# Source and key lists kept in SBUF, and a ScalarE copy in place of each group's index DMA

## The chip, the cores and the metric

The kernel runs on one core of a Trainium2 chip. The metric is the device time of one execution in microseconds (us), and less is better. Engines are called as in the profile: PE (TensorE matmul, with its weight loads as PEld), DVE (VectorE), ACT (ScalarE), POOL (GpSimd) and SP (SyncE, which here only issues DMAs). A "q" behind a name is that engine's sequencer: waits, register work, DMA issues.

## The reference

Four graph layers over 12,500 nodes with 64 features and 200,000 edges (`src`, `dst`), each followed by a residual sum and a layer norm. The edges are sorted by `dst`.

```python
# layer 0: weighted mean of neighbours
msg = x[src] * edge_weight[:, None];            agg = segment_sum(msg, dst)
# layer 1: messages with edge features
msg = relu(x[src] + edge_attr);                 agg = segment_sum(msg, dst)
# layer 2: x_i and x_j - x_i through one linear map, batch norm, leaky relu
msg = concat([x[dst], x[src] - x[dst]]) @ W.T + b;   h = segment_sum(msg, dst)
# layer 3: graph attention, 8 relations
h = x @ W[r]; s = h @ a_src; d = h @ a_dst
e = leaky_relu(s[src] + d[dst]); alpha = segment_softmax(e, dst)
out += segment_sum(alpha[:, None] * h[src], dst) + bias[r]
```

## The kernel before

The edges are cut into G = 196 groups of 1,024 (128 partitions by S = 8). Each layer begins with a pass over all groups that gathers the rows of the source nodes and sums them by destination. These are passes 0, 1, 2 and 3; a later pass reads back what pass 3 kept, and dense stages stand between the passes. Every pass is a loop of IT = 49 turns with Q = 4 groups in a turn, and group g uses slot q = g mod 4 of `gat` (gathered rows) and `idx` (eight int32 row numbers on each partition).

A gather pass works like this:

- **POOL** (`gather_pass`) waits until the slot's row numbers are there (`s_idx[q]`) and the slot is free (`s_free[q]`), and issues eight indirect DMAs (line 486), one for each of the eight columns. Each of them fetches 128 rows.
- **SP** (`refill`, line 286) waits for `s_free[q]` and then loads the next row numbers of that slot, a DMA of 4 KB from `src_p`, or from `key_d` in pass 3. `first_indices` (line 292) does so for the first four groups of passes 1 to 3.
- **DVE and PE** consume a group. In passes 0 to 2 DVE multiplies or adds (L1005, L1058), makes a one-hot matrix of the destinations in two halves (L931), PE multiplies it with the messages (L679, 8 matmuls), and DVE adds the result to `sum_t` (L937). One `p_sum` bank and one `oh` buffer are used, so that these steps follow each other. The slot is freed by DVE after L1005 (pass 0), by ACT after its Relu (L563, pass 1) or by DVE after the sum (pass 2).
- **Pass 3** has two chains that share no data. ACT waits for a group's gathers, stores the slot to `he_d` (L623), copies one column into `trip` (L625) and then frees the slot of the group before (`free_slot`). DVE and PE meanwhile work from the destination row `drow`: a one-hot by nodes (L1193), 8 matmuls (L793), a selection (L1196, L1200) and a sum (L1202), for each "window" of 128 nodes that the group touches, 293 windows in all. SP feeds both chains in a fixed order: for each group it waits for `s_drused` (DVE has finished a group), issues `dst_row` (L396), then waits for `s_free[q]` and issues the index DMA.

The code that sets this order on SP in pass 3:

```python
def pass3(it, final):
    for q in range(Q):
        if not (final and q >= Q - 2):
            wait_reg(sp, s_drused, it * Q + (q + 1))
            dst_row(q % 2, it * Q + (q + 2))
        if not final:
            refill(3, q, it, key_d)
```

The kernel's functions that the diff touches:

Of the kernel before, what the change touches and what calls it, by code (L numbers as in the profile page):

```python
# [5 lines left out]
P, S = 128, 8  # L6
# [3 lines left out]
Q = 4  # L10
# [26 lines left out]
def program(nc, x, src_p, dst_p, type_p, weight_p, dst_f, type_f, edge_attr, weights, out):  # L37
# [5 lines left out]
    he_d = dram("he_d", (G, P, S * HROW))  # L43
    key_d = dram("key_d", (P, G, S), i32)
    dst16_d = dram("dst16_d", (EP,), i16)
# [4 lines left out]
    with ExitStack() as ctx:  # L50
# [49 lines left out]
        src_i, type_i, dst_i = [trip_flat.bitcast(i32)[:, k * T:(k + 1) * T] for k in range(3)]  # L100
        dstn_i = scan_flat.bitcast(i32)[:, 0:T]
        dst16 = scan_flat[:, 2 * T:2 * T + T // 2].bitcast(i16)
        stat_i = oh[0:SG, :, :, :].rearrange("p a s w -> p (a s w)")[:, 0:2 * GE].bitcast(i32)
# [158 lines left out]
        def _(sp):  # L262
            flat = "p g s -> p (g s)"
            sp.dma_start(stat_i, dst_f.rearrange("(a g e) -> g a e", a=2, g=SG)).then_inc(s_load[0], 16)
            sp.dma_start(dst_i, dst_p.rearrange(flat)).then_inc(s_load[1], 16)
# [23 lines left out]
            def first_indices(n, source):  # L289
                for q in range(Q):  # L290
                    sp.wait_ge(s_free[q], IT * n + 1)
                    sp.dma_start(idx[:, q, :], source[:, q, :]).then_inc(s_idx[q], 16)

# [72 lines left out]

            with sp.Fori(0, IT - 1) as it:
                for q in range(Q):
                    refill(0, q, it, src_p)
            sp.wait_ge(s_keyst, 32)  # L370
            dense_io(0)

            first_indices(1, src_p)
            ea_d = edge_attr.rearrange("(g p s) d -> g p (s d)", p=P, s=S)
# [3 lines left out]
            with sp.Fori(0, IT - 1) as it:  # L378
                for q in range(Q):
                    refill(1, q, it, src_p)  # L380
# [4 lines left out]
            first_indices(2, src_p)  # L385
            with sp.Fori(0, IT - 1) as it:
                for q in range(Q):
                    refill(2, q, it, src_p)
            dense_io(2)
            dense_io(3)  # L390
            dense_io(4)

            first_indices(3, key_d)

# [72 lines left out]
        def _(pool):  # L467
# [27 lines left out]
            pool.wait_ge(s_table, 4)  # L495
            pool.wait_ge(s_keyst, 32)
            gather_pass(3, rel_d, HROW)
# [29 lines left out]
        def _(act):  # L527
            def square_root(n, b, k, per):
# [5 lines left out]
                else:  # L534
                    nc.scalar.activation(r1[:, :], r1[:, :], ACT.Sqrt).then_inc(s_sqrt[n], 1)

            act.wait_ge(s_vconst, 2)
            act.wait_ge(s_sum[0], 1)
# [20 lines left out]

            with act.Fori(0, IT) as it:  # L560
                for q in range(Q):
                    wait_reg(act, s_pre, it * Q + (q + 1))
                    nc.scalar.activation(msg[:, q % 2, :, 0:D], ea[:, q, :, :], ACT.Relu).then_inc(s_msg, 1)  # L563
                    wait_reg(act, s_msg, it * Q + (G + q + 1))
                    act.sem_inc(s_free[q], 1)

            def hidden(it, u, b):
# [51 lines left out]

            with act.Fori(0, IT) as it:  # L620
                for q in range(Q):
# [5 lines left out]
                    if q:  # L627
                        free_slot(q - 1, it)
                free_slot(Q - 1, it)
            act.wait_ge(s_scan_copy, G)  # L630
            act.sem_inc(s_trip, 1)
# [212 lines left out]
        def _(dve):  # L844
# [21 lines left out]
            ch.start()  # L866
            dve.wait_ge(s_load[0], 16)
            ch.add(vec.tensor_reduce(out=ends_g[:, 0, :], in_=stat_i, op=ALU.min, axis=AX.X))
# [10 lines left out]
            dve.sem_inc(s_cols, 1)  # L879
            dve.wait_ge(s_load[1], 16)  # L880
            vec.memset(dstf[:, G, :], 0.0)
# [34 lines left out]

            dve.wait_ge(s_load[3], 48)
# [565 lines left out]
```

## Time and profile before

| | us |
|---|---|
| median of 3 runs (12548.62 to 12606.76) | 12603.83 |
| the profiled execution, by the same clock | 12571.97 |
| its span | 12570.2 |
| busy in it: POOL / PE / DVE / ACT | 6491.1 / 3621.9 / 3237.4 / 329.6 |

The span is 1.8 us shorter than the execution's own time. POOL's busy time counts an indirect DMA as busy for as long as POOL makes its descriptors. No engine is busy for more than 52% of the span. So the page's first part does not say what limits the kernel, and the four gather passes have to be read one by one.

### The profile page before, as it was taken

The numbers are of one execution on the slowest core, as the hardware profiler recorded it, in microseconds if no ns is written. First come the engines' busy times: TensorE is split into PE (matmuls) and PEld (weight loads), VectorE is DVE, ScalarE is ACT, GpSimd is POOL, SyncE is SP. The second block draws the span as 40 slices with busy tenths as digits, with TensorE's granted clock in tenths as the row PEclk, the third lists the DMA queues.
The fourth block names the chain that finished last, engine by engine and source line by source line (L and its number), as shares of the span: only waits on it lengthen the run. The fifth ranks groups of instructions, "written<-read, shape, count | busy, mean of one in ns | idle before, by whom it ended". The sixth has DMA issues, their size and how long they took to land.

```text
span 12570.2 us, 99249 instructions
## 1 busy us (share of the span) xinstructions
PE 3621.9 (29%) x17244; PEld 2968.1 (24%) x17245; DVE 3237.4 (26%) x5805; ACT 329.6 (3%) x648; POOL 6491.1 (52%) x6716
## 2 busy tenths in 40 slices
PE   2222222242222222432232223640000000003558
PEld 2222222242222222322222222220000000002555
DVE  2111211141111111221111111322222222286554
ACT  0000000010000000000000000100000000000000
POOL 6666666525556566346666665035555555402443
PEclk6555555555555555555555555555555555556885
DMA  1111111111111111111111111232222222302220
GB/s 41 21 21 21 20 21 21 20 37 40 40 41 41 41 42 41 37 27 22 22 22 22 22 22 23 65 100 64 64 65 65 64 66 66 64 0 48 72 71 19
DMA packets 620736, 509.88 MB, mean 41 GB/s; under 512 B 405721, under 2 KB 405721, under 8 KB 620574
## 3 DMA queue, kind: packets, MB, share of 16 engines
q0 software_dynamic: 200704, 212.34, 9.2%
q1 hardware_dynamic: 391778, 239.40, 7.5%
q10 hardware_dynamic: 28224, 57.82, 1.2%
q8 instruction: 9, 0.15, 0.0%
q14 instruction: 21, 0.17, 0.0%
HBM read 405.06 MB, written 103.99 MB: 40 GB/s over the span
## 4 chain that ended last, share of the span: by engine, by line
another core or an unknown queue 32%; issue 21%; DVE 16%; DVEq 15%; PE 14%; ACT 1%; DMA 1%; POOL 0%; ACTq 0%; POOLq 0%; SPq 0%; PEldq 0%
PE p_sum L679 6%; DVEq L213 5%; DVE oh L931 3%; DVEq L931 2%; DVE oh L945 2%; DVEq L926 1%; DVEq L209 1%; PE p_a L777 1%; DVEq L1193 1%; DVEq L1189 1%; DVE sel L1196 1%; DVE sel L1200 1%; DVE msg L1005 1%; PE p_sum L834 1%
## 5 line engine op out<-in xcount | busy, mean ns | idle before, releaser
L486 POOL DMA_INDIRECT gat<-x_d,idx x3136 | 3034.9, 968 | 2241.3 <-DMA idx<-in_src_p 1272.4
L679 PE MATMUL p_sum<-oh,msg 128*66 128x128 f32 (+1 forms) x6272 | 1410.8, 418 | 3681.1 <-DVE oh L931 1676.8
L486 POOL DMA_INDIRECT gat<-rel_d,idx x1568 | 1492.0, 952 | 1612.6 <-DMA idx<-key_d 1079.3
L679 PEld LDWEIGHTS p_sum<-oh,msg 128*66 128x66 f32 (+1 forms) x6272 | 1269.7, 227 | 3821.7 <-DVE oh L931 2910.5
L486 POOL DMA_INDIRECT gat<-in_x,idx x1568 | 1532.4, 977 | 1001.8 <-DMA idx<-in_src_p 526.5
L937 DVE TENSOR_TENSOR sum_t<-sum_t,p_sum 64x128 f32 (+1 forms) x588 | 165.0, 281 | 5204.9 <-remote 4100.1
L679 PE MATMUL p_sum<-oh,gat 128*64 128x128 f32 x3136 | 687.5, 410 | 1723.1 <-DVE oh L931 1184.6
L679 PEld LDWEIGHTS p_sum<-oh,gat 128*64 128x64 f32 x3136 | 616.6, 219 | 1793.8 <-DVE oh L931 1219.6
L931 DVE SCALAR_TENSOR_TENSOR oh<-dstf,fine_col,iota 128x512 f32<-128x512 f32 x1176 | 835.0, 748 | 510.2 <-issue 406.1
L793 PE MATMUL p_sum<-trip_s,oht 128*128 x2344 | 202.0, 237 | 2410.9 <-DVE oht L1193 1255.6
L793 PEld LDWEIGHTS p_sum<-trip_s,oht 128*128 128x128 bf16 x2344 | 168.8, 166 | 2445.6 <-issue 2445.6
L811 PE MATMUL p_sum<-oh,msg 128*72 128x128 f32 x3136 | 460.2, 310 | 866.3 <-POOL msg L508 862.2
L811 PEld LDWEIGHTS p_sum<-oh,msg 128*72 128x72 f32 x3136 | 412.6, 166 | 913.8 <-issue 913.8
L506 POOL TENSOR_TENSOR msg<-gat,edge_w 128x512 f32<-128x512 f32 x196 | 205.0, 1046 | 771.0 <-DMA gat<-he_d 527.7
L1196 DVE TENSOR_TENSOR sel<-p_sum,toh 128x384 f32<-128x384 f32 x293 | 163.4, 558 | 877.7 <-remote 451.8
L1193 DVE TENSOR_SCALAR oht<-drow,node_col 128x1024 bf16<-128x1024 int16 x293 | 148.6, 507 | 624.1 <-issue 456.9
L945 DVE SCALAR_TENSOR_TENSOR oh<-dstf,fine_col,iota 128x512 f32<-128x512 f32 x394 | 277.6, 744 | 4.9
L508 POOL TENSOR_TENSOR msg<-toh,edge_w 128x64 f32<-128x64 f32 x196 | 124.9, 637 | 239.3 <-DVE oh L945 239.3
L1058 DVE TENSOR_TENSOR ea<-ea,gat 128x512 f32<-128x512 f32 x196 | 136.4, 696 | 231.2 <-issue 228.1
L563 ACT ACTIVATE msg<-ea 128x512 f32<-128x512 f32 x196 | 123.4, 630 | 2421.3 <-DVE ea L1058 2150.5
L834 PE MATMUL p_sum<-w_wcat,xt 64*128 64x512 f32 x196 | 172.4, 1069 | 0.0
L777 PE MATMUL p_a<-w_wcat,xt 64*128 64x512 f32 x196 | 172.1, 1067 | 0.0
(240 smaller groups left out, 3061.1 us busy)
## 6 DMA issues: line engine op xcount, KB each, us to landing
he_d<-gat ACTq DMA_DIRECT2D x196, 288.0 KB
gat<-he_d SPq DMA_DIRECT2D x196, 288.0 KB, 2.8
ea<-in_edge_attr SPq DMA_DIRECT2D x196, 256.0 KB
gat<-x_d,idx POOLq DMA_INDIRECT x3136
drow<-dst_d SPq DMA_DIRECT2D x196, 256.0 KB
rel_d<-sum_t SPq DMA_DIRECT2D x14, 2016.0 KB, 6.4
gat<-in_x,idx POOLq DMA_INDIRECT x1568
gat<-rel_d,idx POOLq DMA_INDIRECT x1568
```

The source lines that it names most:

```text
L213: v = eng.value_load(win[0:1, table, bass.ds(g, 1)], min_val=0, max_val=(NW * G << 16) - 1)
L486: nc.gpsimd.indirect_dma_start(out=gat[:, q, s, 0:width], out_offset=None, in_=table, in_offset=bass.IndirectOffsetOnAxis(ap=idx[:, q, s:s ...
L506: nc.gpsimd.tensor_tensor(msg[:, q % 2, :, 0:D], gat[:, q, :, 0:D], by_tile(alpha, D), ALU.mult)
L679: ins = nc.tensor.matmul(p_sum[0:width, 0, 0:W], lhs(q, s), oh[:, 0, s, :], start=(s == 0), stop=(s == S - 1))
L777: ins = nc.tensor.matmul(p_a[:, k, :], tile(xt, u, t, D), wt["wcat"][:, :], start=True, stop=True)
L793: ins = nc.tensor.matmul(p_sum[:, 0, s * 6 * R:(s + 1) * 6 * R], oht_tile[:, :, s], table, start=True, stop=True)
L811: ins = nc.tensor.matmul(p_sum[0:HROW, u, 0:W], msg[:, u, s, :], oh[:, u, s, :], start=(s == 0), stop=(s == S - 1))
L834: ins = nc.tensor.matmul(p_sum[:, k, :], tile(xt, u, t, D), wt["wcat"][:, :], start=True, stop=True)
L931: vec.scalar_tensor_tensor(out=oh[:, 0, h * half:(h + 1) * half, :], in0=bc(dst.unsqueeze(2), P, half, W), scalar=fine_col[0:P, bass.ds(at ...
L945: ins = vec.scalar_tensor_tensor(out=oh[:, u, h * half:(h + 1) * half, :], in0=bc(dst.unsqueeze(2), P, half, W), scalar=fine_col[0:P, bass ...
L1193: vec.tensor_scalar(oht[:, :], drow[:, q % 2, :], node_col[:, bass.ds(w, 1)], None, ALU.is_equal).then_inc(s_oh[3][0], 1)
L1196: ch2(vec.tensor_tensor(sel[:, :, :, :].rearrange("p s c (k r) -> p s (c k) r", k=3), p_sum[0:P, 0, 0:S * 6 * R].rearrange("p (s c r) -> p ...
```

## The change

The lists of all source rows (`src_i`) and of all keys (source times 8 plus type, now `key_i`, which has a place of its own in `trip_s`) stay in SBUF. They have 1,568 int32 on each partition. The 784 index DMAs of SP are gone, and so is the round trip of the keys through `key_d`. ACT now waits for `s_free[q]` and copies the group's eight columns into `idx[:, q, :]`; the copy counts `s_idx[q]` up by 1. POOL waits for `s_idx[q]` alone. In passes 0 and 2 ACT does nothing else (`all_indices`); in pass 1 the copy stands behind the Relu of the same slot, in pass 3 behind `free_slot`. On SP the waits for `s_free` remain in pass 1 only, ahead of the load of `edge_attr`. The source list is the first DMA of the program.

```diff
+            sp.dma_start(src_i, src_p.rearrange(flat)).then_inc(s_load[1], 16)
...
-            for q in range(Q):
-                sp.dma_start(idx[:, q, :], src_p[:, q, :]).then_inc(s_idx[q], 16)
-            sp.dma_start(src_i, src_p.rearrange(flat)).then_inc(s_load[3], 16)
...
-            sp.dma_start(key_d.rearrange(flat), src_i).then_inc(s_keyst, 16)
...
-            def refill(n, q, it, source):
-
-                wait_reg(sp, s_free[q], it + (2 + IT * n))
-                sp.dma_start(idx[:, q, :], source[:, bass.ds(it * Q + (Q + q), 1), :]
-                             .rearrange("p a s -> p (a s)")).then_inc(s_idx[q], 16)
...
                     if not (final and q >= Q - 2):
                         wait_reg(sp, s_drused, it * Q + (q + 1))
                         dst_row(q % 2, it * Q + (q + 2))
-                    if not final:
-                        refill(3, q, it, key_d)
...
-                        wait_reg(pool, s_idx[q], it * 16 + 16 * (1 + IT * n))
-                        wait_reg(pool, s_free[q], it + (1 + IT * n))
+                        wait_reg(pool, s_idx[q], it + (1 + IT * n))
...
+            def give_indices(n, q, it, rows_of):
+
+                wait_reg(act, s_free[q], it + (1 + IT * n))
+                nc.scalar.activation(idx[:, q, :], rows_of[:, bass.ds(it * (Q * S) + q * S, S)], ACT.Copy)\
+                    .then_inc(s_idx[q], 1)
...
+            act.wait_ge(s_load[1], 16)
+            all_indices(0)
...
                     nc.scalar.activation(msg[:, q % 2, :, 0:D], ea[:, q, :, :], ACT.Relu).then_inc(s_msg, 1)
                     wait_reg(act, s_msg, it * Q + (G + q + 1))
                     act.sem_inc(s_free[q], 1)
+                    if not final:
+                        give_indices(1, q, act.snap(it + 1), src_i)
...
+            all_indices(2)
...
                     if q:
                         free_slot(q - 1, it)
+                        if not final:
+                            give_indices(3, q - 1, act.snap(it + 1), key_i)
                 free_slot(Q - 1, it)
+                if not final:
+                    give_indices(3, Q - 1, act.snap(it + 1), key_i)
...
-            ch.add(vec.scalar_tensor_tensor(out=src_i, in0=src_i, scalar=float(R), in1=type_i, op0=ALU.mult, op1=ALU.add))
+            ch.add(vec.scalar_tensor_tensor(out=key_i, in0=src_i, scalar=float(R), in1=type_i, op0=ALU.mult, op1=ALU.add))
```

Two places show how the queues change. The first is SP in the loop of pass 3. Before the change, half a turn of it reads (L396 is `dst_row`, L286 the index DMA; an ISA or REGISTER_ALU row is register work, with the wait that stands on it):

```order
L396 ISA [waits s_drused]
L396 DMA drow<-dst_d 128x1024
L209 REGISTER_ALU
L286 ISA [waits s_free0]
L286 DMA idx<-key_d 128x8
L396 ISA [waits s_drused]
L396 DMA drow<-dst_d 128x1024
L286 ISA [waits s_free1]
L286 DMA idx<-key_d 128x8
```

After it the same stretch reads (`dst_row` is line 371 there):

```order
L385 ISA
L371 ISA [waits s_drused]
L371 DMA drow<-dst_d 128x1024
L371 ISA [waits s_drused]
L371 DMA drow<-dst_d 128x1024
```

The index load has left the queue in which it stood behind the wait for DVE, and `dst_row` no longer stands behind the wait for a free slot.

The second place is ACT in the same loop. Before the change (L623 is the store, L625 the copy into `trip`):

```order
L623 ISA [waits s_gat1]
L623 DMA he_d<-gat 128x576
L625 ISA
L625 ACTIVATE trip<-gat 128x8
L209 ISA [waits s_scan_copy]
L623 ISA [waits s_hest0,s_gat2]
L623 DMA he_d<-gat 128x576
```

After it (the store is line 621, the copy into `trip` 623, the index copy 511):

```order
L621 ISA [waits s_gat1]
L621 DMA he_d<-gat 128x576
L623 ISA
L623 ACTIVATE trip<-gat 128x8
L208 ISA [waits s_scan_copy]
L208 REGISTER_ALU [waits s_hest0]
L511 ISA [waits s_free0]
L511 ACTIVATE idx<-trip_s 128x8
L621 ISA [waits s_gat2]
L621 DMA he_d<-gat 128x576
```

The index copy of slot 0 for the next turn stands right behind the freeing of slot 0 and ahead of the wait for the gathers of slot 2. No instruction of DVE or PE is waited for between them.

## Rows read from the trace of the kernel before

**Rows 1.** Stretches of the four gather passes: length, busy us (count), PEclk, DMA share, GB/s

```profile
11.00:2537.00 2526.00, 705.92 (x3126) 634.12 (x3127) 507.65 (x1018) 0.00 (x0) 1532.43 (x1568) 0.57 0.12 22
2718.00:5228.00 2510.00, 685.01 (x3072) 617.47 (x3072) 453.45 (x768) 120.88 (x192) 1520.15 (x1568) 0.57 0.18 41
5423.00:7813.00 2390.00, 681.09 (x3104) 610.95 (x3104) 338.39 (x583) 0.00 (x0) 1514.72 (x1568) 0.57 0.12 22
8331.00:10936.00 2605.00, 201.98 (x2344) 168.79 (x2344) 588.92 (x1387) 43.90 (x197) 1492.03 (x1568) 0.50 0.27 65
```

**Rows 2.** Waits of POOL in passes 0, 1, 2, 3: us in total, times, longest

```profile
POOL gat L486 <- DMA idx<-in_src_p: 526.5, 62, 10.7
...
POOL gat L486 <- DMA idx<-in_src_p: 696.2, 68, 182.1
...
POOL gat L486 <- DMA idx<-in_src_p: 576.1, 61, 196.0
...
POOL gat L486 <- DMA idx<-key_d: 1079.3, 62, 519.2
```

**Rows 3.** Timeline of pass 0: start us, busy us, engine, what [idle before <-releaser]

```profile
2007.99 0.95 POOL L486 DMA_INDIRECT gat<-in_x,idx  x1 [8.70 <-DMA idx<-in_src_p]
...
2022.25 0.68 DVE L1005 TENSOR_TENSOR msg<-gat,edge_w 128x512 f32<-128x512 f32 x1
...
2024.44 3.68 PE L679 MATMUL p_sum<-oh,msg 128*66 128x128 f32 x16 [6.07 <-issue]
...
2037.42 0.95 POOL L486 DMA_INDIRECT gat<-in_x,idx  x1 [0.30 <-issue]
2042.07 0.28 DVE L937 TENSOR_TENSOR sum_t<-sum_t,p_sum 66x128 f32 x1 [17.02 <-remote]
...
2043.41 0.68 DVE L1005 TENSOR_TENSOR msg<-gat,edge_w 128x512 f32<-128x512 f32 x1
2044.48 0.33 SPq L286 DMA_DIRECT2D idx<-in_src_p  x1
...
2047.09 0.95 POOL L486 DMA_INDIRECT gat<-in_x,idx  x1 [8.72 <-DMA idx<-in_src_p]
```

**Rows 4.** Line 210 between 2044 and 2048: the waits' ends on each sequencer

```profile
L210 POOLq EVENT_SEMAPHORE  x2: 17/17/17, 2046.2 to 2046.3; - x2
```

**Rows 5.** Timeline of pass 1, ACT behind DVE

```profile
4009.70 0.69 DVE L1058 TENSOR_TENSOR ea<-ea,gat 128x512 f32<-128x512 f32 x1 [1.63 <-issue]
...
4010.51 0.63 ACT L563 ACTIVATE msg<-ea 128x512 f32<-128x512 f32 x1 [22.51 <-DVE ea L1058]
```

**Rows 6.** Line 625, ACT's column copy: duration ns min/median/max, first and last start

```profile
L625 ACT ACTIVATE trip<-gat x196: 217/217/222, 8344.2 to 10920.3; 128x8 f32 x196
```

**Rows 7.** Waits of SP's queue in pass 3: us in total, times, longest

```profile
SPq L210 <- DVEq L1203: 1017.6, 99, 22.7
```

**Rows 8.** Timeline of pass 3, DVE: two windows, POOL gathering and pausing

```profile
9498.71 0.23 DVE L1202 TENSOR_TENSOR trip<-trip,sel 128x16 f32 x1 [0.15 <-issue]
...
9521.11 0.18 DVE L1202 TENSOR_TENSOR trip<-trip,sel 128x16 f32 x1 [0.16 <-issue]
...
9525.36 0.18 DVE L1202 TENSOR_TENSOR trip<-trip,sel 128x16 f32 x1 [0.15 <-DVE sel L1200]
```

**Rows 9.** Line 1202 in pass 3: one execution for each window

```profile
L1202 DVE TENSOR_TENSOR trip<-trip,sel x293: 174/176/239, 8361.3 to 10934.9; 128x16 f32 x147
```

**Rows 10.** Line 1202, the first 5 us of POOL's 96 runs in pass 3

```profile
sum 435.30, DVE 15.01; mean DVE 0.16
```

**Rows 11.** Line 1202, from 10 to 20 us in POOL's runs (66 stretches)

```profile
sum 651.20, DVE 10.51; mean DVE 0.16
```

**Rows 12.** Line 1202, later than 20 us in POOL's runs (35 stretches)

```profile
sum 441.60, DVE 3.27; mean DVE 0.09
```

**Rows 13.** Timeline at the start of pass 1

```profile
2716.02 1.78 SPq L292 DMA_DIRECT2D idx<-in_src_p  x4
...
2718.63 0.95 POOL L486 DMA_INDIRECT gat<-x_d,idx  x1 [182.06 <-DMA idx<-in_src_p]
```

More of the change, by code:

```diff
@@ L100, in program @@
         src_i, type_i, dst_i = [trip_flat.bitcast(i32)[:, k * T:(k + 1) * T] for k in range(3)]
-        dstn_i = scan_flat.bitcast(i32)[:, 0:T]
-        dst16 = scan_flat[:, 2 * T:2 * T + T // 2].bitcast(i16)
+        dstn_i, key_i = scan_flat.bitcast(i32)[:, 0:T], scan_flat.bitcast(i32)[:, 2 * T:3 * T]
+        dst16 = scan_flat[:, T:T + T // 2].bitcast(i16)
         stat_i = oh[0:SG, :, :, :].rearrange("p a s w -> p (a s w)")[:, 0:2 * GE].bitcast(i32)
@@ L263, in _ @@
             flat = "p g s -> p (g s)"
+            sp.dma_start(src_i, src_p.rearrange(flat)).then_inc(s_load[1], 16)
             sp.dma_start(stat_i, dst_f.rearrange("(a g e) -> g a e", a=2, g=SG)).then_inc(s_load[0], 16)
[L265 removed]
+            sp.dma_start(dst_i, dst_p.rearrange(flat)).then_inc(s_load[0], 16)
             sp.dma_start(edge_w[:, 0:G, :].rearrange(flat), weight_p.rearrange(flat)).then_inc(s_load[2], 16)
[L267 to L269 removed]
             sp.dma_start(type_i, type_p.rearrange(flat)).then_inc(s_load[3], 16)
@@ L279, in _ @@
             sp.wait_ge(s_key, 1)
-            sp.dma_start(key_d.rearrange(flat), src_i).then_inc(s_keyst, 16)
             sp.dma_start(dst16_d.rearrange("(p t) -> p t", p=P), dst16).then_inc(s_keyst, 16)
-            def refill(n, q, it, source):
-                wait_reg(sp, s_free[q], it + (2 + IT * n))
-                sp.dma_start(idx[:, q, :], source[:, bass.ds(it * Q + (Q + q), 1), :]
-                             .rearrange("p a s -> p (a s)")).then_inc(s_idx[q], 16)
[L289 to L292, printed above, removed]
             def dense_io(n):
@@ L364, in dense_io @@
                 sp.sem_inc(s_table, 1)
[L367 to L370, printed above, removed]
             dense_io(0)
-            first_indices(1, src_p)
             ea_d = edge_attr.rearrange("(g p s) d -> g p (s d)", p=P, s=S)
@@ L379, in _ @@
                 for q in range(Q):
-                    refill(1, q, it, src_p)
+                    wait_reg(sp, s_free[q], it + (2 + IT))
                     sp.dma_start(ea_slot[q], ea_d[bass.ds(it * Q + (Q + q), 1), :, :]
@@ L383, in _ @@
             dense_io(1)
[L385 to L388, printed above, removed]
             dense_io(2)
@@ L391, in _ @@
             dense_io(4)
-            first_indices(3, key_d)
             def dst_row(u, g):
@@ L535, in square_root, with first_indices, all_indices @@
                     nc.scalar.activation(r1[:, :], r1[:, :], ACT.Sqrt).then_inc(s_sqrt[n], 1)
+            def give_indices(n, q, it, rows_of):
+                wait_reg(act, s_free[q], it + (1 + IT * n))
+                nc.scalar.activation(idx[:, q, :], rows_of[:, bass.ds(it * (Q * S) + q * S, S)], ACT.Copy)\
+                    .then_inc(s_idx[q], 1)
+            def first_indices(n, rows_of):
+                for q in range(Q):
+                    act.wait_ge(s_free[q], 1 + IT * n)
+                    nc.scalar.activation(idx[:, q, :], rows_of[:, q * S:(q + 1) * S], ACT.Copy).then_inc(s_idx[q], 1)
+            def all_indices(n):
+                first_indices(n, src_i)
+                with act.Fori(1, IT) as it:
+                    for q in range(Q):
+                        give_indices(n, q, it, src_i)
+            act.wait_ge(s_load[1], 16)
+            all_indices(0)
             act.wait_ge(s_vconst, 2)
@@ L558, in _, with relu_groups @@
             two_step(act, stage_in(0, D + 2), roots(0, 2))
-            with act.Fori(0, IT) as it:
+            def relu_groups(it, final):
                 for q in range(Q):
@@ L565, in _ @@
                     act.sem_inc(s_free[q], 1)
+                    if not final:
+                        give_indices(1, q, act.snap(it + 1), src_i)
+            first_indices(1, src_i)
+            with act.Fori(0, IT - 1) as it:
+                relu_groups(it, False)
+            relu_groups(IT - 1, True)
             def hidden(it, u, b):
@@ L618, in free_slot, with keep_rows @@
                 act.sem_inc(s_free[q], 1)
-            with act.Fori(0, IT) as it:
+            def keep_rows(it, final):
                 for q in range(Q):
@@ L628, in _ @@
                         free_slot(q - 1, it)
+                        if not final:
+                            give_indices(3, q - 1, act.snap(it + 1), key_i)
                 free_slot(Q - 1, it)
+                if not final:
+                    give_indices(3, Q - 1, act.snap(it + 1), key_i)
+            act.wait_ge(s_key, 1)
+            first_indices(3, key_i)
+            with act.Fori(0, IT - 1) as it:
+                keep_rows(it, False)
+            keep_rows(IT - 1, True)
             act.wait_ge(s_scan_copy, G)
@@ L866, in _ @@
             ch.start()
-            dve.wait_ge(s_load[0], 16)
+            dve.wait_ge(s_load[0], 32)
             ch.add(vec.tensor_reduce(out=ends_g[:, 0, :], in_=stat_i, op=ALU.min, axis=AX.X))
@@ L915, in _ @@
                                p_b[0:D, 0, 0:2 * R].rearrange("d (r c) -> d c r", c=2)))
-            dve.wait_ge(s_load[3], 48)
+            dve.wait_ge(s_load[1], 16)
+            dve.wait_ge(s_load[3], 32)
             vec.memset(typef[:, G, :], 0.0)
             ch.add(vec.tensor_copy(typef[:, 0:G, :].rearrange("p g s -> p (g s)"), type_i))
-            ch.add(vec.scalar_tensor_tensor(out=src_i, in0=src_i, scalar=float(R), in1=type_i, op0=ALU.mult, op1=ALU.add))
+            ch.add(vec.scalar_tensor_tensor(out=key_i, in0=src_i, scalar=float(R), in1=type_i, op0=ALU.mult, op1=ALU.add))
             ch(vec.tensor_copy(dst16, dstn_i))
```

3 lines of the change are left out of this document (removed).

## The prediction

> **What bounds the kernel now.** I read the stretches of the passes first, then POOL's waits, then one cycle of a pass in the timeline, and last how fast pass 3's two chains go at different moments. The four gather passes take 2,526, 2,510, 2,390 and 2,605 us [rows 1], together 10,031 of 12,570. In each of them POOL issues 1,568 gathers. Its busy time and the 0.30 us ahead of each [rows 3] add up to 1,492 + 470 = 1,962 us in pass 3 and about 2,000 in pass 0: that is POOL's floor, 10.0 us for a group of eight. The rest is stops. In passes 0, 1 and 2 POOL waits 62, 67 and 60 times for a group's index DMA (without the one wait at the start of passes 1 and 2, 182.1 and 196.0 us), 8.5, 7.7 and 6.3 us each [rows 2].
>
> One stop of pass 0 shows what it is made of [rows 3]. POOL started at 2007.99 and issued 24 gathers, three groups. PE's matmuls for one group start at 2024.44 and are busy for 3.68 us, yet DVE's addition behind them starts at 2042.07, 17.02 us after DVE's last work. Nothing that the timeline shows lies between. It starts 3.7 us after POOL's last gather (2037.42 + 0.95 = 2038.37), because POOL has no free slot left and falls silent. DVE then finishes its multiplication at 2043.41 + 0.68 = 2044.09, which frees a slot. SP issues the index DMA at 2044.48, and POOL gathers again at 2047.09. So a stop of 8.7 us is 3.7 us until PE's end reaches DVE, 2.0 us of DVE and 3.0 us from the free slot to the gather. I read from this that a long unbroken run of gathers holds PE and DVE up, and that a silence of POOL lets them go on.
>
> Pass 3 shows the same from the other side. I split it by the time since POOL began a run (a run ends with a stop of over 1 us; there are 96). Line 1202 runs once per window, 0.176 us each, 293 times [rows 9], so its busy time counts windows. In a run's first 5 us DVE does 15.01 / 0.176 = 85 windows in 435.3 us, 0.196 per us [rows 10]; from 10 to 20 us 60 in 651.2, 0.092 per us [rows 11]; later than 20 us 18.6 in 441.6, 0.042 per us [rows 12]. Single windows agree: one that ended at 9521.11 came 22.4 us after the one before, under a run that ended meanwhile, and the next came 4.25 us later with POOL silent [rows 8].
>
> **Passes 0 to 2.** The change takes out SP's issue and the DMA: 2047.09 - 2044.09 = 3.0 us per stop. In their place come four things. ACT wakes behind another engine's end 4010.51 - 4010.39 = 0.12 us later [rows 5]. Its register work for the address I take as 0.1 us (no row of before has just this; 0 to 0.5). The copy of 128 x 8 elements takes 0.217 us in the nearest row, a column copy of the same size [rows 6]. POOL needs 0.8 us from its last wait (2046.3, [rows 4]) to the gather, as now; with one wait fewer perhaps 0.1 less. With 0.1 us for the two semaphores that is 1.4 us, and a stop gets 1.6 us shorter. The bounds are 1.0 (register work and semaphores slow down) and 2.0 us (only copy and POOL's 0.8 count). Over 189 stops it gives 302 us (189 to 378). In 2,000 us between stops the indices are there before POOL asks, today and after, so nothing is won there. The index transfers themselves I value at nothing: pass 1 has 196 more SP transfers, of `edge_attr`, than pass 0, and is 16 us shorter [rows 1].
>
> The gain holds as long as a run stays at three groups. POOL needs its third group's slot 20 us after the start of the run. That slot was freed at 2022.25 + 0.68 = 2022.9, or 14.9 us in; starting 1.6 us earlier puts this at 16.5, and the copy at 17. Three us are left.
>
> At the start of passes 1 to 3 the first copies are done long before, where today 2.6 us lie between SP's issue and the gather [rows 13]: 1.5 us saved three times, 5 us. At the program's start the list of 784 KB goes first, in place of index loads that stood behind three such DMAs; I take no change.
>
> **Pass 3.** ACT's copy is not what matters here. Today SP's index DMA stands behind `dst_row` and its wait for DVE: SP waits 1,017.6 us for DVE's group ends [rows 7]. POOL can therefore run only about four groups ahead of DVE, and whenever DVE falls behind, POOL stops and DVE catches up. After the change POOL waits for ACT alone. ACT frees a slot one group after its gathers, so the indices come some 20 us before POOL asks for them. POOL should run nearly unbroken, 196 x 10.0 = 1,962 us, with a few stops 2,000. DVE and PE then stand under a run older than 20 us all the time: 2,000 x 0.042 = 84 windows. The other 209 follow with POOL silent, at 0.196 per us: 1,066 us. Pass 3 would take 3,066 us, 461 more than now. The rate has the fewest windows behind it (18.6), so I bound it: 0.03 gives 233 windows left and 3,189 us; 0.092 gives 109 left and 2,556. The break-even for the whole change is where pass 3 lasts 2,605 + 307 = 2,912: 2,000 + (293 - 2,000 r) / 0.196 gives r = 0.057.
>
> **The sum**, against the profiled execution's own 12,572 us: -302 - 5 + 461 = +154, so 12,726, rounded to 12,730. The median of the runs is 12,604, 0.3% above that execution; against it the forecast is 1.0% slower.
>
> **The rivals.**
> 1. *ACT becomes the brake of pass 3* (0.24). The copy and its wait lengthen ACT's work per group. If ACT is held up by long runs too (this trace has no such row for it, since POOL always stops), POOL still pauses, and DVE goes at something between 0.055 and 0.092: pass 3 takes 2,556 to 2,934 us and the kernel 12,220 to 12,590. Against it speaks the slack of two groups.
> 2. *DVE keeps its pace* (0.16). Over the whole of pass 3 it does 293 windows in 2,605 us, 0.1125 per us [rows 1, 9], and it no longer waits for a `dst_row` stuck behind a slot. With 225 windows done in POOL's 2,000 us and 68 left, pass 3 takes 2,347 us, and the kernel 12,572 - 307 - 258 = 12,007. It needs the fall from 0.196 to 0.042 to come from SP's order and not from POOL's runs. In passes 0 to 2, where SP has no such order, PE's end reaches DVE late too, which speaks against it.
> 3. *No hold-up at all* (0.05). If POOL's runs and DVE's slowness only coincide, DVE needs 293 / 0.196 = 1,495 us and hides behind POOL's 2,000: pass 3 loses 605 us and the kernel takes 11,660. The Trainium skill ("SBUF — State Buffer", section "Who interferes with whom") says that only the port pair shared by DVE and GpSimd causes contention, and that PE never has to wait for another engine. By that rule this rival would hold for PE. The trace disagrees: 17.02 us between PE's 3.68 us of work and DVE's addition, and a rate that falls by a factor of 4.7.
> 4. *The third group slips* (0.06). If the copy comes more than 3 us later than I think under a run, runs of passes 0 to 2 end after two groups: (20.1 + 7.1) / 2 = 13.6 us per group in place of 12.9, over 588 groups +410 us in place of -302. The kernel would take 13,440.
> 5. *Nothing moves* (0.04): POOL's stops last until PE's end is through anyway, and ACT's late copy gives pass 3 its old pauses back. 12,572.
>
> The forecast keeps 0.45, with a range of its own of 12,520 (saving 378, rate 0.055) to 12,960 (saving 189, rate 0.03). A measurement tells about 0.5%, 63 us, from no change. Faster: 0.15 of rival 1, rivals 2 and 3: 0.36. Same: 0.09 of rival 1 and rival 5: 0.13. Slower: the forecast and rival 4: 0.51. The range runs from rival 2 to above the forecast's bound, 12,000 to 12,960; rivals 3 and 4 stay out.
>
> **What the profile after would show.** In passes 0 to 2: as many stops, 7.1 us in place of 8.5 in pass 0, and ACT copies of 0.22 us 0.3 us behind each freed slot. In pass 3: the last gather some 2,000 us after the first, hardly a stop over 1 us, fewer than 120 executions of the window's sum by then, and a stretch of about 1,000 us without gathers in which DVE does a window every 5.1 us. The prediction is wrong if DVE has done over 180 windows when POOL ends, if POOL takes over 2,300 us because it waits for ACT, or if the number of stops in passes 0 to 2 changes by more than a tenth.

## The result and the profile after

The changed kernel takes 12,847.2 us (median of 4 runs, 12,815.2 to 12,865.7), the kernel before in the same sitting 12,597.9 (4 runs). The ratio is 1.020, with a 95% interval of 1.017 to 1.024: the change costs 2%. The profiled execution of after is its quickest, 12,815.2 with a span of 12,812.7 us, 242.5 more than the span of before.

The stretches of the four gather passes, from POOL's first gather to the last gather or window (columns as in [rows 1]: length, busy us and count of PE, PEld, DVE, ACT and POOL, then granted clock, DMA share, GB/s):

```profile
6.00:2439.00 2433.00, 708.77 (x3120) 632.58 (x3120) 509.35 (x1017) 40.05 (x193) 1525.42 (x1568) 0.58 0.12 23
2625.00:5038.00 2413.00, 695.39 (x3088) 623.82 (x3088) 456.81 (x772) 161.53 (x385) 1512.14 (x1568) 0.56 0.19 43
5220.00:7531.00 2311.00, 681.94 (x3088) 609.34 (x3088) 337.51 (x579) 39.98 (x192) 1521.05 (x1568) 0.57 0.12 22
8063.00:11178.00 3115.00, 202.30 (x2344) 168.82 (x2344) 581.78 (x1386) 84.21 (x393) 1486.64 (x1568) 0.50 0.21 54
```

Against [rows 1], passes 0, 1 and 2 are 93, 97 and 79 us shorter and pass 3 is 510 us longer. Pass 3 begins 268 us earlier, and 510 - 268 = 242. So the whole difference lies in the gather passes, shorter in passes 0 to 2 and longer in pass 3, as was predicted.

Where pass 3 loses its time is seen in the page's 40 slices (320 us each; each digit is the busy share in tenths):

```profile
DVE  2221121331111112211111113211111133386554
POOL 6666666356666664466666630566666600001443
```

In slices 27 to 32 POOL gathers and DVE shows a 1. In the next three (33 to 35) POOL shows 0 and DVE 3. Line 1210 (line 1202 before) runs once per window. Its executions in the two parts of pass 3, in the columns length, busy us (count), clock, DMA share, GB/s:

```profile
8063.00:10284.00 2221.00, 21.78 (x122) 0.50 0.26 62
10284.00:11178.00 894.00, 30.02 (x171) 0.50 0.11 33
```

While POOL gathers, 2,220 us long, DVE gets through 122 windows, 0.055 per us. In the 894 us after the last gather it does the other 171, 0.191 per us. Before the change the two chains ended together: POOL's last gather was at 10917.5 and the last window at 10935.0.

I split pass 3 again by the time since POOL began a run. These are sum rows of line 1210, first for the first 5 us of the 58 runs, then from 10 to 20 us (33 stretches), last for what is older than 20 us (24 stretches):

```profile
sum 281.80, DVE 5.02; mean DVE 0.09
...
sum 316.00, DVE 2.00; mean DVE 0.06
...
sum 1077.10, DVE 8.21; mean DVE 0.34
```

At 0.1785 us each (21.78 / 122), the last row holds 46 windows in 1,077 us, 0.043 per us; [rows 12] gave 0.042. Two things have changed. Much more time is spent there, 1,077 us in place of 442. And DVE is slow in young runs too: 28 windows in 282 us are 0.10 per us, where [rows 10] gave 0.196, and 11 in 316 us are 0.035, where [rows 11] gave 0.092. At the rates of before, the three rows would hold 129 windows; they hold 85. So the age of a run alone does not set DVE's pace.

The timeline shows the hold-up on single windows. Here POOL gathers without a stop, then pauses for 5.6 us, then gathers again:

```profile
8540.83 0.18 DVE L1210 TENSOR_TENSOR trip<-trip,sel 128x16 f32 x1 [0.23 <-issue]
...
8557.67 0.17 DVE L1210 TENSOR_TENSOR trip<-trip,sel 128x16 f32 x1 [0.15 <-issue]
...
8564.83 0.21 ACT L511 ACTIVATE idx<-trip_s 128x8 int32 x1 [6.26 <-issue]
...
8565.85 0.94 POOL L458 DMA_INDIRECT gat<-rel_d,idx  x1 [5.63 <-ACT idx L511]
...
8569.68 0.17 DVE L1210 TENSOR_TENSOR trip<-trip,sel 128x16 f32 x1 [0.15 <-issue]
...
8575.25 0.18 DVE L1210 TENSOR_TENSOR trip<-trip,sel 128x16 f32 x1 [0.15 <-DVE sel L1208]
...
8591.93 0.18 DVE L1210 TENSOR_TENSOR trip<-trip,sel 128x16 f32 x1 [0.15 <-issue]
```

The windows follow 16.8, 12.0, 5.6 and 16.7 us behind each other, and the 5.6 is the one right behind the pause. The pause itself was made by ACT: its copy at 8564.83 came behind 6.26 us of "issue", time in which it waited for nothing that the profile shows. POOL's waits for this copy in passes 0, 1, 2 and 3 (us in total, times, longest), to be held against [rows 2]:

```profile
POOL gat L458 <- ACT idx L511: 401.0, 58, 9.5
...
POOL gat L458 <- ACT idx L511: 417.9, 71, 10.8
...
POOL gat L458 <- ACT idx L511: 303.6, 64, 7.6
...
POOL gat L458 <- ACT idx L511: 249.5, 49, 10.7
```

In pass 0 the waits shrank from 8.5 to 6.9 us each, in pass 3 from 560 us (1,079.3 less the one of 519.2) to 250.

### The profile page after: what moved, and what is told of

The parts are those of the page before. It is cut to its first block and busy times, and to the rows that moved or that the text cites. A ratio compares the mean times of both kernels' runs of the same rounds, so it can differ in the third digit from the quotient of the medians.

```text
span 12812.7 us, 97715 instructions
## 1 busy us (share of the span) xinstructions
PE 3635.9 (28%) x17244; PEld 2971.4 (23%) x17245; DVE 3232.5 (25%) x5805; ACT 492.6 (4%) x1433; POOL 6476.4 (51%) x6716
## 5 line engine op out<-in xcount | busy, mean ns | idle before, releaser
L511 ACT ACTIVATE idx<-trip 128x8 int32 x576 | 120.0, 208 | 4704.6 <-issue 2172.6
L1194 DVE TENSOR_TENSOR toh<-typef,rel_col 128x64 f32<-128x64 f32 x196 | 44.3, 226 | 858.2 <-issue 588.3
```

## The experiments

The kernels ran in eight sittings (the one of the result is the first), each with the kernel before among them. The sittings are of two kinds, and the kernel before tells them apart. It took 12,563 to 12,601 us in five of them, and 10,508 to 10,519 us in the other three. In no sitting did it change from one to the other. I call them held and free sittings; why is seen in experiment 1.

| sitting | kernel before, us | what ran |
|---|---|---|
| 1, held | 12,597.9 | the change |
| 2, free | 10,508.0 | e1, e2, e3, e4 |
| 3, held | 12,569.5 | a1, the change again |
| 4, free | 10,519.0 | b1, b3, b4 |
| 5, held | 12,584.8 | c3 |
| 6, free | 10,517.6 | c5 |
| 7, held | 12,563.4 | d5 |
| 8, held | 12,600.8 | f4 |

Theory: a long unbroken run of gathers holds up what the other engines' sequencers do. In passes 0 to 2 the change only makes POOL's stops shorter. In pass 3 it takes out the stops in which DVE caught up. The first rival is that DVE is slow in pass 3 for another reason (SP's order, ACT's copies, or POOL being busy at all). The second is that nothing is held up.

**1. Each half of the change alone (e1, e2).** e1 keeps the ACT copies in passes 0 to 2 and gives pass 3 its old index DMAs back; e2 is the reverse.

```diff
# e1, on top of the change
+            sp.dma_start(key_d.rearrange(flat), key_i).then_inc(s_keyst, 16)
...
+            for q in range(Q):
+                sp.wait_ge(s_free[q], IT * 3 + 1)
+                sp.dma_start(idx[:, q, :], key_d[:, q, :]).then_inc(s_idx[q], 16)
...
+                    if not final:
+                        wait_reg(sp, s_free[q], it + (2 + IT * 3))
+                        sp.dma_start(idx[:, q, :], key_d[:, bass.ds(it * Q + (Q + q), 1), :]
+                                     .rearrange("p a s -> p (a s)")).then_inc(s_idx[q], 16)
...
-                        if not final:
-                            give_indices(3, q - 1, act.snap(it + 1), key_i)
...
# e2, on top of the change
...
+            with sp.Fori(0, IT - 1) as it:
+                for q in range(Q):
+                    refill(0, q, it, src_p)
...
-            all_indices(0)
...
-            all_indices(2)
```

> Passes 0 to 2 as changed, pass 3's index DMAs back on SP behind the wait for DVE. Theory (order on SP held POOL back for DVE's good): passes 0 to 2 keep their gain of 268 us, pass 3 takes its old 2,605 us, so 12,300 us (12,250 to 12,360), faster than both kernels. Rival (pass 3 is slow for another reason, such as where the keys lie or the copies of passes 0 to 2): pass 3 stays above 3,000 us and the kernel above 12,750.

> The mirror image: index DMAs in passes 0 to 2 as before, ACT's copies in pass 3 alone. Theory: passes 0 to 2 as before, pass 3 at 3,110 us, so 13,080 us (13,000 to 13,150). Rival (the two parts are not independent): outside that range, near 12,600 if the loss needs both.

Both ran in free sitting 2: e1 took 10,502.8 us (0.9996, interval 0.9986 to 1.0006), e2 10,514.4 (1.0008, 0.9999 to 1.0018). Neither half does anything there. POOL's waits in e2 over the whole execution show why:

```profile
POOL gat L483 <- issue: 1919.6, 6268, 9.5
```

and the stretch of pass 3, by the columns of the first fence:

```profile
6903.00:8872.00 1969.00, 202.34 (x2344) 168.80 (x2344) 585.51 (x1386) 82.40 (x387) 1490.56 (x1568) 0.50 0.34 85
```

Of 6,272 gathers 6,268 follow the one before without waiting for any engine. A pass is one run of 1,568 gathers at POOL's floor of 10.0 us a group, which the change does not touch. DVE's windows go on at full pace under it. The sequencer's register step and the window's sum (ns, shortest, median, longest; first and last start):

```profile
L1229 DVEq FUSED_REGOPS  x293: 69/69/75, 6926.4 to 8463.5; - x147
L1229 DVE TENSOR_TENSOR trip<-trip,sel x293: 174/175/177, 6926.5 to 8463.6; 128x16 f32 x147
```

293 windows in 1,537 us are 0.191 per us, the rate that the changed kernel reached in the held sitting only when POOL had gone silent; they end 408 us before POOL does. Both runs miss the times that the theory gave (12,300 and 13,080 us), which were worked out from held executions. This is what rival 3 of the prediction describes, in sittings other than the one that was asked about. These runs tell nothing of how the halves do in a held sitting. b1, e1 once more, met a free sitting again:

> Passes 0 to 2 as changed, pass 3's index DMAs back on SP behind the wait for DVE, hoped for on a chip that shows the hold-up (the kernel before near 12,600 us). Theory: passes 0 to 2 keep their gain of 268 us and pass 3 takes its old 2,605 us: 12,300 us (12,250 to 12,360), ratio 0.98. Rival (pass 3 is slow for another reason than POOL's freedom): above 12,750. If the kernel before takes near 10,508 us here, both say 10,500 and nothing is told.

It took 10,514.4 us against 10,519.0 (0.9996, 0.9986 to 1.0006). So e1 and e2 were never seen in a held sitting, and neither was the change as a whole ever seen in a free one.

**2. A bound on POOL's lead in pass 3 (e3, b3, c3).** The changed kernel, but in pass 3 POOL waits before each group until it is at most four groups ahead of DVE. No index DMA comes back, and SP's order stays as after the change.

```diff
                         wait_reg(pool, s_idx[q], it + (1 + IT * n))
+                        if n == 3:
+                            wait_reg(pool, s_keyst, it * Q + (q + 17))
...
+            dve.sem_inc(s_keyst, 4)
...
                     dve.sem_inc(s_drused, 1)
+                    dve.sem_inc(s_keyst, 1)
```

> The change whole, with ACT's copies in all passes, and one wait more: in pass 3 POOL gathers a group only when DVE has finished the group four before it. Theory (POOL's unbroken runs hold DVE and PE up): pass 3 falls to 2,450 to 2,600 us, fewer than ten runs over 40 gathers, and the kernel takes 12,150 to 12,300 us. Rival (ACT's extra work in pass 3, or the copies as such, slow DVE): pass 3 stays near 3,110 and the kernel near 12,850.

> The change whole, and in pass 3 POOL gathers a group only when DVE has finished the group four before it. Where the kernel before takes near 12,600 us, theory: pass 3 falls from 3,110 to 2,450 to 2,600 us, and the kernel takes 12,150 to 12,300 us. Rival (ACT's copies in pass 3 slow DVE by themselves): near 12,850. Where it takes near 10,508, both say 10,510.

> The same kernel as before it: ACT's copies in all passes, and in pass 3 POOL gathers a group only when DVE has finished the group four before it. Where the kernel before takes near 12,600 us, theory: pass 3 falls from 3,110 to 2,450 to 2,600 us, the kernel takes 12,150 to 12,300 us, ratio 0.965 to 0.98. Rival (ACT's copies slow DVE in pass 3 by themselves): near 12,850, ratio 1.02. Where it takes near 10,508, both say 10,510.

In the free sittings 2 and 4 it took 10,510.2 and 10,520.9 us (1.0003 and 1.0001, both intervals hold 1). In held sitting 5 it took 12,197.0 us against 12,584.8: 0.970 (0.966 to 0.975). One wait added to the changed kernel turns a loss of 2% into a gain of 3%. Its passes 0 to 2 last 2,431, 2,438 and 2,311 us, together 246 us less than in [rows 1], so their gain is there without pass 3's loss. The stretch of pass 3:

```profile
8083.00:10550.00 2467.00, 202.06 (x2344) 168.89 (x2344) 582.96 (x1386) 83.94 (x389) 1502.02 (x1568) 0.50 0.27 68
```

POOL's waits in it:

```profile
POOL gat L460 <- DVEq L1215: 425.8, 88, 12.8
...
POOL gat L460 <- DMA dst_d<-trip_s: 20.1, 7, 3.6
```

Pass 3 now lasts 2,467 us in place of 3,115, although POOL waits for DVE 88 times, 426 us together. 289 of the 293 windows are done when POOL ends. POOL's gathers take 230 us longer than after the change (2,450 against 2,220), and the tail of 894 us is down to 17. That is the theory's mark: the cure for DVE is to make POOL wait. ACT's copies and SP's order are as in the change, so neither of them is what made DVE slow.

**3. The change again (a1).**

> The changed kernel once more, beside the kernel before. In the four runs ahead of this one the kernel before took 10,508 us in place of 12,598, and its twins gathered without a single stop. Theory (the loss and the gain both come from PE and DVE being held up under long runs of gathers): if the kernel before takes about 10,508 us here too, there is nothing to lose or gain in the loops, POOL's floor sets all passes, and the changed kernel lies 10 to 30 us below it (earlier starts of the passes), a ratio of 0.997 to 1.0; if it takes about 12,600 us, the ratio is 1.02 again. Rival (the change costs something by itself, whatever the hold-up): 1.01 or more in both cases.

In held sitting 3 the change took 12,838.0 us against 12,569.5: 1.0215 (1.019 to 1.024). Again 123 windows fall within POOL's 2,218 us and 170 within the 892 us behind. The result stands in a second held sitting.

**4. POOL busy without gathers (e4, b4, f4).** In pass 3 POOL issues no gathers; in their place it fills a scratch row of 1,024 elements eight times per group, each time waiting for itself. The gathers of pass 3 are left out, with the traffic that they make, and ACT takes up a group when POOL has counted it. The rest stays.

```diff
-            gather_pass(3, rel_d, HROW)
...
+            with pool.Fori(0, IT) as it:
+                for q in range(Q):
+                    wait_reg(pool, s_idx[q], it + (1 + IT * 3))
+                    for s in range(S):
+                        nc.gpsimd.iota(busy_row, pattern=[[1, 2 * S * D]], base=0, channel_multiplier=0, **exact)\
+                            .then_inc(s_pch, 1)
+                        wait_reg(pool, s_pch, it * (Q * S) + (q * S + s + 1))
+                    pool.sem_inc(s_keyst, 1)
...
-                    wait_reg(act, s_gat[q], it * 128 + 128 * (1 + 3 * IT))
+                    wait_reg(act, s_keyst, it * Q + (q + 17))
```

> Leaves out pass 3's gathers: POOL fills a scratch tile eight times per group (1,024 elements per partition, about as long as a gather) and then tells ACT, which stores and copies what lies in the slots. The output is not the reference's. Theory (it is the gathers, not a busy POOL, that hold PE and DVE up): DVE does its 293 windows at about 0.19 per us while POOL is busy, pass 3 takes 1,600 to 2,100 us and the kernel 11,300 to 11,800. Rival (any long busy stretch of POOL does it): fewer than 0.08 windows per us and a kernel of 12,700 or more.

> Leaves out pass 3's gathers: POOL fills a scratch tile eight times per group in their place, and ACT stores and copies what lies in the slots. Where the kernel before takes near 12,600 us, theory (the gathers hold PE and DVE up, a busy POOL does not): 293 windows at about 0.19 per us, pass 3 at 1,600 to 2,100 us and the kernel at 11,300 to 11,800. Rival (any long busy stretch of POOL does it): under 0.08 windows per us, the kernel at 12,700 or more.

> Leaves out pass 3's gathers (POOL fills a scratch tile eight times per group in their place, ACT stores and copies what lies in the slots). Where the kernel before takes near 12,600 us, theory (the gathers hold PE and DVE up, a busy POOL does not): about 0.19 windows per us in pass 3, which takes 1,600 to 2,100 us, and a kernel of 11,500 to 11,900 us. Rival (any long busy stretch of POOL does it): under 0.08 windows per us, the kernel at 12,700 or more. Where it takes near 10,510, both say 10,420.

In the free sittings it took 10,410.9 and 10,419.6 us (one run each); nothing is held up there under gathers either, so by themselves these two tell nothing apart. In held sitting 8 it took 11,612.3 against 12,600.8 (one run each). Its pass 3, first POOL's fills:

```profile
L477 POOL IOTA ea<- 128x1024 f32 x1568 | 1560.2, 995 | 319.5 <-POOL ea L477 314.3 <-ACT idx L530 5.2
```

the window's sum and the step of the sequencer ahead of it:

```profile
L1223 DVEq FUSED_REGOPS  x293: 69/69/75, 8128.2 to 9751.3; - x147
L1223 DVE TENSOR_TENSOR trip<-trip,sel x293: 175/176/177, 8128.3 to 9751.4; 128x16 f32 x147
```

and DVE's wait for PE:

```profile
DVE sel L1217 <- PE p_sum L814: 392.6, 292, 1.4
```

POOL is as busy as with gathers (995 ns for each of 1,568 fills; a gather has 948), yet DVE does 293 windows in 1,623 us, 0.181 per us, and never waits more than 1.4 us for PE's end. The small rest to 0.191 is in DVE's own work, its one-hot over the nodes. Its row here, and the one of e2 under gathers in a free sitting:

```profile
L1214 DVE TENSOR_SCALAR oht<-drow,node_col 128x1024 bf16<-128x1024 int16 x293 | 235.8, 805 | 226.8 <-DVE toh L1207 137.2
...
L1220 DVE TENSOR_SCALAR oht<-drow,node_col 128x1024 bf16<-128x1024 int16 x293 | 149.6, 510 | 226.8 <-DVE toh L1213 137.2
```

It takes 805 ns in place of 510, and 293 times 295 ns are the 86 us by which these windows take longer than e2's. The fills in the free run e4 give the same: 804 ns, and 293 windows in 1,623 us. So a POOL busy with fills makes one of DVE's instructions longer, but the pass that is held up under gathers runs under fills as it does in a free sitting. It takes the indirect DMAs, with what they set going, to hold DVE up; whether POOL's making of them or their transfers do it, this run does not tell.

**5. A bound in all passes (c5, d5).** POOL may be at most two groups ahead of DVE, in passes 0 to 2 as well.

```diff
                         wait_reg(pool, s_idx[q], it + (1 + IT * n))
+                        if n < 3:
+                            wait_reg(pool, s_acc, it * Q + (q + 1 + G * n))
+                        if n == 3:
+                            wait_reg(pool, s_keyst, it * Q + (q + 17))
...
+            dve.sem_inc(s_acc, 2)
+            dve.sem_inc(s_keyst, 2)
...
-                    vec.tensor_tensor(part, part, p_sum[0:width, 0, 0:W], ALU.add).then_inc(s_acc, 1)
+                    vec.tensor_tensor(part, part, p_sum[0:width, 0, 0:W], ALU.add)
...
+                        dve.sem_inc(s_acc, 1)
```

> ACT's copies everywhere, and POOL may gather a group only when DVE has finished the group two before it, in all four passes (four before it, in pass 3 alone, in the last kernel, which took 12,197 us). Theory (unbroken runs hold PE and DVE up, and a short silence lets them catch up at little cost): where the kernel before takes near 12,600 us, runs in passes 0 to 2 end after 8 or 16 gathers, the 16 us hold-ups of DVE go, a group takes 11 to 11.8 us in place of 12.2, and the kernel takes 11,700 to 12,050 us. Rival (each silence costs its 3.5 us whatever the length of the run ahead of it): two stops where one was, 12,300 to 12,700. Where it takes near 10,508, POOL's floor no longer hides DVE's chain: 10,510 to 10,700.

> The kernel with the gate at two groups in all passes once more. Where the kernel before takes near 12,600 us, theory: 11,700 to 12,050 us, runs of 8 or 16 gathers in passes 0 to 2 and no hold-up of DVE over 10 us. Rival (every silence costs the same): 12,300 to 12,700. Where it takes near 10,520 us, as in the run ahead of this one: 1.003 again.

In free sitting 6 it took 10,550.0 us against 10,517.6: 1.0031 (1.002 to 1.004). Where nothing is held up, the waits only cost. In held sitting 7 it took 12,054.8 against 12,563.4: 0.959 (0.957 to 0.962), the best kernel there. Its four passes:

```profile
6.00:2398.00 2392.00, 710.94 (x3152) 639.97 (x3152) 518.18 (x1027) 40.03 (x193) 1535.09 (x1568) 0.59 0.12 24
2570.00:4938.00 2368.00, 705.37 (x3120) 635.12 (x3120) 458.63 (x780) 162.84 (x387) 1516.93 (x1568) 0.57 0.18 44
5108.00:7403.00 2295.00, 706.39 (x3120) 635.36 (x3120) 344.68 (x585) 39.99 (x192) 1505.84 (x1568) 0.58 0.12 23
7921.00:10418.00 2497.00, 202.04 (x2344) 168.78 (x2344) 581.89 (x1386) 83.89 (x389) 1494.87 (x1568) 0.50 0.26 67
```

Passes 0 to 2 gain 41, 45 and 16 us more against the change, with shorter runs (82 of pass 0's 114 are of two groups). The mechanism came as expected in passes 0 and 1: DVE's longest idle stretch ahead of its addition falls from 17.6 and 33.1 us to 8.7 and 9.3 (in pass 2, 106 of them are still over 10 us). The size did not: a group takes 12.2, 12.1 and 11.7 us (12.4, 12.3 and 11.8 after the change), where 11 to 11.8 were expected, and the time lies 5 us above the expected range. Shorter runs help, but the stops that make them short eat much of it: 113 of 3.7 us in pass 0, in place of 82 of 5.5. That is near the 3.5 us that the rival puts on a stop, though its time is missed by far. In pass 3 the bound of two groups is no better than that of four (2,497 us against 2,467).

## Why the prediction was right in sign and range, and where it was wrong

The sign was forecast at 0.51, and the time of 12,847 lies 117 us above the forecast of 12,730 but inside the range. The change costs twice what was forecast, 2.0% in place of 1.0%. Term by term, against the profiled execution:

| term | forecast, us | measured, us |
|---|---|---|
| passes 0 to 2, from first to last gather | -302 | -270 |
| starts of the program and of passes 1 to 3 | -5 | +1 |
| pass 3, to the last window | +461 | +511 |
| sum | +154 | +242 |

**A stop of 7.1 us: right.** A cycle of pass 0 after the change, beginning with a stop:

```profile
1273.78 0.68 DVE L1013 TENSOR_TENSOR msg<-gat,edge_w 128x512 f32<-128x512 f32 x1
1274.81 0.21 ACT L511 ACTIVATE idx<-trip 128x8 int32 x1 [19.49 <-DVEq L1016]
...
1275.82 0.94 POOL L458 DMA_INDIRECT gat<-in_x,idx  x1 [6.89 <-ACT idx L511]
...
1283.55 3.68 PE L687 MATMUL p_sum<-oh,msg 128*66 128x128 f32 x16 [3.90 <-issue]
1294.39 0.28 DVE L945 TENSOR_TENSOR sum_t<-sum_t,p_sum 66x128 f32 x1 [10.23 <-remote]
...
1296.25 0.68 DVE L1013 TENSOR_TENSOR msg<-gat,edge_w 128x512 f32<-128x512 f32 x1
1297.28 0.21 ACT L511 ACTIVATE idx<-trip 128x8 int32 x1 [14.80 <-issue]
1298.29 0.94 POOL L458 DMA_INDIRECT gat<-in_x,idx  x1 [2.75 <-issue]
```

From the freed slot (1273.78 + 0.68 = 1274.46) to the gather at 1275.82 it is 1.36 us; 1.4 was forecast, and 3.0 it was before. Over all of pass 0, stops over 5 us went from 58 of 8.95 us to 54 of 7.08.

**"As many stops": wrong.** This is the step that I had named as one that would make the prediction wrong. Pass 0 has 82 stops over 1 us in place of 65, pass 1 84 in place of 67, pass 2 77 in place of 69 (84, 81 and 64 in a1, so in pass 2 the number is not steady). The third group of a run has less room than the 3 us that I gave it. The cycle shows it: the run starts at 1275.82, DVE's second addition comes at 1294.39, 18.6 us in, the copy is there at 1297.49, and POOL, which was ready for it at 1298.29 - 2.75 = 1295.54, has to stop. Eleven runs of pass 0 are cut after two groups in this way, but by 2.5 us each and not by a full stop. In the cycle of [rows 3] the second addition came 12.9 us after the run's start at 2007.99:

```profile
2020.90 0.28 DVE L937 TENSOR_TENSOR sum_t<-sum_t,p_sum 66x128 f32 x1 [5.60 <-remote]
```

So rival 4 was right in its place, now and then, and wrong in its price. In pass 0 the stops over 5 us gave back 519 - 382 = 137 us and the short ones took 70 - 15 = 55 of it. The gain in stops is 82 us (534 to 452), where 62 stops by 1.6 us, 99, were forecast.

**The starts** of passes did not gain 5 us. The first gather of the program comes 4.6 us earlier, where no change was forecast. From the last gather of a pass to the first of the next it takes 4.5 us more ahead of pass 1, 12.8 less ahead of pass 2 and 14.5 more ahead of pass 3, where 1.5 less was forecast each time. Ahead of pass 3 it is 534 us here, 525 in c3 and 519 in d5 and in the kernel before, so it moves with more than the copies. Why is open.

**Pass 3: the coupling right, the rates and the runs only in part, and luck in the sum.** What held was that POOL is no longer held back for DVE and leaves it behind, and the rate under a run older than 20 us, 0.043 against 0.042. "Hardly a stop over 1 us" was wrong: there are 57, of 4.8 us on average, 49 of them waits for ACT's copy, and POOL takes 2,220 us in place of 2,000. Only 1,077 us of it lie beyond the twentieth microsecond of a run, not all. The slack of two groups that I gave ACT against rival 1 was not enough, because ACT is held up as well. The rows of register steps on ACT's and DVE's sequencers in pass 3 (ns, shortest, median and longest), first ACT's of before, then the two of after:

```profile
L625 ACTq FUSED_REGOPS  x196: 15/46/709, 8344.1 to 10920.3; - x196
...
L511 ACTq FUSED_REGOPS  x192: 3/69/1398, 8092.3 to 10246.5; - x192
...
L1210 DVEq FUSED_REGOPS  x293: 14/69/1387, 8086.7 to 11177.5; - x147
```

DVE's step takes 69 ns, and in the rows of e2 and f4 never more than 75; after the change it takes up to 1.4 us. The prediction says that the trace of before has no row for a held-up ACT. The first row above is one: a step of 46 ns that takes up to 709. So ACT brakes POOL a little, which is rival 1's mechanism, but not far enough. With POOL's 2,220 us, 0.191 behind it and the 268 us that the rest gained (2,603 + 268 = 2,871), the rate would have to be (293 - (2,871 - 2,220) x 0.191) / 2,220 = 0.076 for the change to cost nothing, and it was 0.055. 122 windows were done by POOL's end (forecast: 84, and "fewer than 120"), and 894 us without gathers followed (1,066). POOL's part is 220 us longer than forecast and the tail 172 shorter; these make the term's 50.

That these two nearly cancel is luck. There is a second piece of luck. The prediction let DVE's rate hang on the age of a run alone. Had that been so, the 1,143 us of POOL's part that are not in runs older than 20 us (its stops included) would have held many more than the 76 windows that they held. By the rates that the trace of before gives for ages of up to 5, 10 and 20 us and for the stops (0.195, 0.153, 0.088 and 0.100 per us), DVE would have done about 198 windows by POOL's end and pass 3 would have lasted some 2,717 us; the kernel would then have been faster than before by some 155 us. That is an estimate. So with the runs as they came, the loss took something that the prediction does not have: DVE slow in young runs as well. One difference that could be behind it, not tested: before, a stop of POOL ended when DVE had finished a group; now it ends when ACT comes through, wherever DVE is. In the stops of before, 639 us, 64 windows ended; in those of after, 271 us, 10; in those of c3, where POOL waits for DVE again, 92 in 497 us.

By the table, the misses are 50 us in pass 3, 32 in the stops of passes 0 to 2 and 6 in the starts, all of one sign.

**Rival 2** (DVE keeps its pace, because SP's order made it slow) is out: DVE did 122 windows by POOL's end and not 225, and SP's order is the same in the change and in c3, where the bound on POOL's lead made DVE quick. (Something of it shows in the free sitting: in e1, which has SP's old order, the last window starts 14 us before POOL's end, in e2 it ends 408 us before it. It costs no time there.) **Rival 3** is out for held sittings and the case in free ones. The rule weighed there (the Trainium skill, "SBUF — State Buffer", section "Who interferes with whom": only the port pair of DVE and GpSimd contends, and a DMA never contends with a compute engine) agrees with every trace of a free sitting and with f4, where DVE's one-hot takes 805 ns in place of 510 beside POOL's fills. It does not account for the held sittings, where PE's end reached DVE 7.2 us late in the cycle above (1294.39 against 1283.55 + 3.68) and 14 in [rows 3]. (The 17.02 us that the prediction sets against PE's 3.68 are DVE's idle time; from PE's end it is 2042.07 - 2028.12 = 13.95.)

That long runs cost DVE time in held sittings is shown, by c3 and d5 (runs made short, DVE quick) and f4 (no gathers, DVE quick). That the change lost its time by taking away POOL's waits for DVE in pass 3 is shown by c3. What holds the sequencers up, why only in some sittings, and why young runs are slow too in the change, is open.

## What to carry to other kernels

An index load that stands behind a wait for another engine can be the only thing that paces a free-running producer. Before it is taken out, ask which chain used the producer's pauses, and if one did, put an explicit bound on the lead in its place; here one wait was worth 5% of the time. A cheaper hand-over shortens each stop, but it also moves the start of the next run ahead of its own consumer, and new stops appear there. Time the kernel before in every sitting: a change that loses 2% in one kind of sitting was worth nothing measurable, in either of its halves, in the other.

## What was not expected of the hardware

**The same kernel takes 20% longer in some sittings.** 10,508 to 10,519 us against 12,563 to 12,601, with nothing in between, and the same kind for all runs of a sitting. Nearly all of it lies in the gather passes: the four take 10,031 us in [rows 1] and 8,001 in e2. I can't tie it to the chip: the chips are numbered in the records, and the numbers 6, 7 and 8 stand in sittings of both kinds (whether a number means the same chip each time I don't know). Nor is it the clock: the granted clock of the window matmuls in pass 3 is 0.50 of full speed, the lower of its two levels (1.2 GHz), in the rows of both kinds of sitting above. In passes 0 to 2 it is a little lower in [rows 1] than in e2 (0.57 against 0.58 to 0.66), but PE is not busy for longer (706, 685 and 681 us against 712, 707 and 704).

**What is slow in a held sitting is the sequencers.** Many of their steps take 0.70 or 1.4 us in place of under 0.1, on ACT, DVE and SP alike. Of the sequencers' records (DMA issues left out) from 8,063 to 10,284 us in the trace of the change, 54% on DVE, 47% on ACT and 15% on SP last over 0.4 us. In the traces of the free sittings no register step or branch does, in any pass; what is longer there are loads of registers and true waits. Nor does one in pass 3 of f4. The engines' own work is unchanged: the window's sum takes 175 ns at the median in both. It took indirect DMAs to bring it about (f4). In the kernel before it got worse with the age of a run, from 0.196 windows per us [rows 10] to 0.042; in the change DVE is at 0.10 in a run's first 5 us already.

**A bound on the lead is a choice for one kind of sitting.** Two groups give 4.1% in held sittings and cost 0.3% in free ones; four groups in pass 3 alone give 3.0% and cost nothing that was measured.
